# One decoder layer on one core: the third norm turned by DMA transposes instead of TensorE, with the router's product and the output sum reordered

## The chip, the cores and the metric

The kernel runs on one core of one Trainium2 chip. The metric is the device time of one execution in microseconds (us), the median of several runs. PE is TensorE, PEld its weight loads, DVE is VectorE, ACT is ScalarE, POOL is GpSimd and SP is SyncE, which issues the DMAs.

## What is computed

Eight sequences of 512 rows by 256 features go through one pre-norm decoder layer:

```
x = x + attn(layernorm(x))        # 16 heads; softmax over the sequence makes a Toeplitz matrix; W_V, W_O, bias
x = x + xattn(layernorm(x), ctx)  # causal cross attention, one head of width 256
x = x + ffn(layernorm(x))         # 2 shared experts and 16 routed ones (64 wide), top 2
# ffn: logits = flat @ router_w; the two largest of 16 are weighed (softmax) into comb
#      h = silu(flat @ wg) * (flat @ wu) * comb ; out = sum over experts of h @ wd
```

Products are computed in three fp16 passes on high and low halves (`three_passes`, L140), so each operand is kept as a high part (ACT copies to fp16) and a low part (the rest, a subtraction on DVE or POOL).

## The kernel before

**Staging.** One batch passes three stages in three consecutive iterations, so iteration `it` holds three batches at once: stage f of batch `it` (first norm, `z`, values), stage m of batch `it-1` (Toeplitz product, output projection, second norm, cross attention, third norm), stage d of batch `it-2` (router, gates, down products). `f, m, d, n` say which stages run; n is the first norm of the next batch. The iterations are 0 to 8, then `finish`. Iteration 0 has f alone and iteration 1 (`second_iteration`) has f and m together with much of the context work (`context(n, units)`: queries and values of the cross attention for batch n); 2 and 3 take the contexts 6 and 7; 4 to 6 are a hardware loop (`Fori`, L452 and PE's own at L2007); 7 has no n; 8 has no f and no n.

**Order.** Every engine has its own hand written program; all order between engines comes from semaphores. A wait holds up everything behind it on its engine. PSUM has three pairs of banks, `turned`, `score` and `rows`, each with a written order of its uses (L58 to L61); PE fills (`fill`) when the use two places before is taken, and DVE takes in that order (`take`, `reach`). Two more banks, `wide`, hold the Toeplitz sums, the contexts and, from `down(b, 0)` on, the output sums y.

**Gates.** For each of ten middle blocks j: PE makes g and u (`gate_up`, 12 matmuls of 512 columns, from h3T), ACT the tanh, DVE `open_gate` (and the product with `comb_rows`, L1252), DVE `pass_gate` (L1260), ACT the high part (L909), POOL the low part (L700), PE `down(j)` (12 matmuls of 256 columns). Block 9 is weighed after it is passed (`weigh_gate`, L1276).

**Third norm.** At j = 7 and j = 8 DVE normalises the halves of h3 (L1139). PE turns h3 in the middle of `gate_up(9)`, 8 transposes of 128x128 fp32 (L1638), between g9 and u9. ACT and DVE then part the turned banks into h3T (L813, L1149). The router's `logits` (L1691) and the next iteration's gates read h3T.

**End of an iteration on PE:** g9, turn h3, u9, `down(7)`, `z_product`, `down(8)`, `logits`, `down(9)`, then the next iteration's Toeplitz quarters. On DVE: pass and weigh block 9, part h3T, `z_max`, `route_top` (waits for the logits), `add_y` (waits for `down(9)`), then `route_rest` and the sums of the Toeplitz quarters. In iteration 8 `add_y` is left out and comes in `finish`, behind `route_top` and ahead of `route_rest`; PE's u0 there waits until DVE has counted two uses of `rows` past (L122), which DVE does behind `route_rest`.

**Second iteration, near its end.** PE: contexts 4, two halves of the turn of h3, `context(5, (0, 1))`, turn h1, `context(5, (2, 3))`. ACT and DVE part h3T, then the units of context 5, then h1T. ACT must wait for the store of context 2 before it writes unit 0 of context 5, which lies in the same buffer (`SAME_PAIR`, L66 and L881).

**Transfers.** SP already turns mix (two `DMA_TRANSPOSE` an iteration, L503) and h1 (one, L510). Its queue is in order.

## Time and profile before

| | us |
|---|---|
| median of 3 runs (lowest, highest) | 569.32 (568.86, 569.55) |
| the profiled execution's own time | 569.86 |
| its span, first to last instruction | 568.1 |
| PE busy | 542.3 (95%) |
| DVE busy | 424.9 (75%) |
| ACT busy | 257.4 (45%) |
| POOL busy | 201.2 (35%) |

A matmul's duration contains its way through the array, so consecutive matmuls overlap: the rate is read from start to start. In a timeline, a row is start, duration, engine, line, operation, output<-inputs, count, and in brackets the engine's idle time before it with what ended it. Iteration 1 begins at 33.84, 2 at 87.81, 3 at 155.67, 5 at 283.41, 6 at 343.90, 7 at 404.39, 8 at 464.46 (first Toeplitz matmul of each).

### The profile page before, as it was taken

The page shows a single profiled execution, that of the slowest core. Times are in us where ns is not written, and L with a number is a line of the kernel's source. Part 1 is how long each engine was busy: PE and PEld are TensorE (multiplying, and loading weights), DVE is VectorE, ACT ScalarE, POOL GpSimd, SP SyncE. Part 2 cuts the span into 40 slices and gives each one's busy share as a digit, 9 for nine tenths or more (in the row PEclk, how much of TensorE's full clock was granted, in tenths as well). Part 3 has the DMA queues.
Part 4 walks back from the last instruction along what each step waited for, and adds up shares of the span by engine and source line. Part 5 has one row for each costly group of instructions (what it writes and reads, how often), then busy time and mean ns, then how long its engine had stood idle before and what let it go on. Part 6 is the DMA issues. An engine that isn't in the chain of part 4 may idle for free. (4 is left out here: it accounts for less than half of the span.)

```text
span 568.1 us, 12928 instructions
## 1 busy us (share of the span) xinstructions
PE 542.3 (95%) x4716; PEld 369.6 (65%) x4716; DVE 424.9 (75%) x1101; ACT 257.4 (45%) x521; POOL 201.2 (35%) x246
## 2 busy tenths in 40 slices
PE   5799889999999999999999999999999998999997
PEld 4576557566776668666776668666866685666455
DVE  5867878778776697778886888678876876777654
ACT  4566657435354445435353545435543334332332
POOL 4225752214522154314512343334421343133123
PEclk9999989999999999999999999999999999999999
DMA  7988696793459823693459643994189216200341
GB/s 241 305 282 304 198 388 201 165 348 117 113 123 269 281 67 84 139 303 121 112 121 270 204 111 78 213 304 111 48 175 324 69 60 132 58 1 1 91 98 38
DMA packets 90734, 94.70 MB, mean 167 GB/s; under 512 B 28224, under 2 KB 76224, under 8 KB 90432
## 3 DMA queue, kind: packets, MB, share of 16 engines
q1 hardware_dynamic: 90688, 94.09, 58.7%
q8 instruction: 29, 0.48, 0.3%
q14 instruction: 17, 0.14, 0.1%
HBM read 75.66 MB, written 12.12 MB: 155 GB/s over the span
## 5 line engine op out<-in xcount | busy, mean ns | idle before, releaser
L700 POOL TENSOR_TENSOR mid<-gated,mid 128x512 f16<-128x512 f32 x72 | 86.4, 1200 | 214.2 <-ACT mid L909 214.1
L909 ACT ACTIVATE mid<-gated 128x512 f16<-128x512 f32 x72 | 45.0, 625 | 83.4 <-DVEq L1268 80.1
L142 PE MATMUL wide<-w_d,mid 128*128 128x256 f16 x288 | 78.5, 273 | 0.0
L144 PE MATMUL wide<-w_d,mid 128*128 128x256 f16 x288 | 78.5, 273 | 0.0
L143 PE MATMUL wide<-w_d,mid 128*128 128x256 f16 x288 | 78.5, 272 | 0.0
L1246 DVE SCALAR_TENSOR_TENSOR gated<-gated,score 128x512 f32<-128x512 f32 x72 | 49.2, 683 | 37.7 <-ACT gated L904 37.4
L142 PE MATMUL rows<-h3T,w_gu 128*128 128x512 f16 x160 | 60.7, 379 | 0.3 <-DVEq L122 0.3
L142 PE MATMUL score<-h3T,w_gu 128*128 128x512 f16 x160 | 60.7, 379 | 0.2
L143 PE MATMUL rows<-h3T,w_gu 128*128 128x512 f16 x160 | 60.6, 379 | 0.0
L144 PE MATMUL rows<-h3T,w_gu 128*128 128x512 f16 x160 | 60.6, 379 | 0.0
L144 PE MATMUL score<-h3T,w_gu 128*128 128x512 f16 x160 | 60.6, 379 | 0.0
L143 PE MATMUL score<-h3T,w_gu 128*128 128x512 f16 x160 | 60.6, 379 | 0.0
L904 ACT ACTIVATE gated<-score 128x512 f32<-128x512 f32 x72 | 42.3, 588 | 35.0 <-PE score L144 35.0
L1260 DVE SCALAR_TENSOR_TENSOR gated<-gated,rows 128x512 f32<-128x512 f32 x72 | 49.1, 682 | 7.5 <-PE rows L144 6.2
L890 ACT ACTIVATE prob<-score,s_bias 128x128 f32<-128x128 f32 (+3 forms) x32 | 16.9, 528 | 71.9 <-DVE s_bias L1213 71.9
L1252 DVE TENSOR_TENSOR gated<-gated,stage 128x512 f32<-128x512 f32 x49 | 33.9, 692 | 2.2 <-DMA stage<-comb_scratch 0.2
L142 PEld LDWEIGHTS wide<-w_d,mid 128*128 128x128 f16 x288 | 28.1, 98 | 10.1 <-issue 3.0
L143 PEld LDWEIGHTS wide<-w_d,mid 128*128 128x128 f16 x288 | 28.2, 98 | 5.8
L670 POOL TENSOR_SCALAR var_eps<-mean_var 128x2 f32<-128x2 f32 (+1 forms) x31 | 10.0, 323 | 61.0 <-DVE mean_var L1130 60.3
L144 PEld LDWEIGHTS wide<-w_d,mid 128*128 128x128 f16 x288 | 28.2, 98 | 3.3
L144 PEld LDWEIGHTS rows<-h3T,w_gu 128*128 128x128 f16 x160 | 15.7, 98 | 18.9
L144 PEld LDWEIGHTS score<-h3T,w_gu 128*128 128x128 f16 x160 | 15.7, 98 | 18.9
(251 smaller groups left out, 1423.5 us busy)
## 6 DMA issues: line engine op xcount, KB each, us to landing
toep<-z_scratch SPq DMA_DIRECT2D x14, 2048.0 KB, 18.0
stage<-comb_scratch SPq DMA_DIRECT2D x32, 512.0 KB, 8.4
toep<-z_scratch SPq DMA_DIRECT2D x4, 1024.0 KB, 10.3
x_bo<-in_x SPq DMA_DIRECT2D x8, 512.0 KB, 11.7
x_in<-in_xr SPq DMA_DIRECT2D x7, 512.0 KB, 11.1
qT<-q_scratch SPq DMA_DIRECT2D x7, 512.0 KB, 3.8
vx<-v_scratch SPq DMA_DIRECT2D x7, 512.0 KB, 5.1
out<-x_out SPq DMA_DIRECT2D x7, 512.0 KB, 3.3
```

Source lines behind the costliest of these rows:

```text
L142: pe.matmul(out, stationary[0], moving[0], start=start, stop=False, **kw)
L143: pe.matmul(out, stationary[0], moving[1], start=False, stop=False, **kw)
L144: return pe.matmul(out, stationary[1], moving[0], start=False, stop=stop, **kw)
L670: pool.tensor_scalar(var_eps[n][:, some], mean_var[n][:, some, 1], EPS, X_H ** -2, ALU.add, ALU.mult).then_inc(eps_added[n].sem, 1)
L700: pool.tensor_tensor(mid_slot(j, 1, late), gate_slot(j, late), mid_slot(j, 0, late), ALU.subtract).then_inc(mid_split.sem, 1)
L890: act.activation(prob[:, c % 2, 0:n], score.bank(score_use(it, c))[:, 0:n], ACT.Exp, bias=s_bias[:, c:c + 1], scale=1 / (X_Q * X_H), accum ...
L904: act.activation(gate_slot(j, late), score.bank(f"g{j}")[:], ACT.Tanh, scale=0.5 / (X_H * X_W)).then_inc(tanh_done.sem, 1)
L909: act.activation(mid_slot(j, 0, late), gate_slot(j, late), ACT.Copy).then_inc(mid_hi.sem, 1)
L1246: dve.scalar_tensor_tensor(to, to, 1.0, score.bank(f"g{j}")[:], ALU.add, ALU.mult).then_inc(score.taken.sem, 1)
L1252: dve.tensor_tensor(to, to, comb_rows[:, j - NSH], ALU.mult).then_inc(opened.sem, 1)
L1260: dve.scalar_tensor_tensor(to, to, X_MID / (2 * (X_H * X_W) ** 2), rows.bank(f"u{j}")[:], ALU.mult, ALU.mult).then_inc(rows.taken.sem, 1)
```

## The change

In iterations 2 to 7 h3 is no longer turned by PE. ACT copies the halves of h3 to fp16 in h2's buffer, DVE takes the low part of the first half and POOL that of the second, and SP turns high and low parts with one DMA transpose each, into h3T (odd iterations) or cT (even ones). Iterations 1 and 8 still turn on PE. On PE the logits go behind `down(9)`, on DVE `add_y` goes ahead of `route_top`. SP issues h1's transpose ahead of the fetch of the context. The iterations 4 to 6 are written out. In iteration 0 ACT and POOL part the columns of context 1 earlier; in iteration 1 ACT, DVE, POOL and PE are reordered.

```
+FIRST_MOVED = 2
...
-            with eng.Fori(2 + len(CONTEXT_IN), B - 1) as it:
+            for it in range(2 + len(CONTEXT_IN), B - 1):
                 iteration(it, True, True, True, True)
...
+            def move_h3(it, b):                                   # SP
+                if it == 2 or it == 4 and not h3_moved(2):
+                    sp.wait_ge(ctx_taken.sem, ctx_taken.at(6, UNITS))
+                sp.wait_ge(rows.ready.sem, rows.is_ready(it - 1, f"u{MID - 1}"))
+                parts_of = h2[:].rearrange("p c e -> p (c e)").bitcast(F16).rearrange("p (a n) -> p a n", a=2)
+                for a, made in enumerate((h3_hi, h3_split)):
+                    hold(sp, made, made.at(b, 2))
+                    sp.dma_start(h3T_of(it)[:, a].rearrange("p k (c s) -> p (k c) s", s=P), parts_of[:, a],
+                                 transpose=True).then_inc(h3T_moved.sem, 16)
...
+                if n and d:
+                    move_h1(it + 1)
                 if f and m:
                     fetch_context(it, it)
-                if n and d:
-                    move_h1(it + 1)
+                if h3_moved(it):
+                    move_h3(it, it - 1)
...
                 reciprocal_deviation(it - 1, 2)                   # POOL, second_iteration
+                part_context_columns(5)
                 reciprocal_deviation(it - 1, 2, 1)
-                part_context_columns(5)
...
                 for j in range(MID):                              # POOL
+                    if h3_moved(it) and j == MID - 2:
+                        part_h3(it - 1, 1)
                     if d and j:
                         part_mid(it - 2, j)
-                    if f and not m and j == 2:
+                    if f and not m and j == 0:
                         part_context_columns(1)
...
+                    if h3_moved(it - 1):                          # ACT, take_rest, q == 0
+                        act.wait_ge(h3T_moved.sem, h3T_moved.at(it - 2, 32))
...
-                exp_scores(it, it - 1, 2)                         # ACT, second_iteration
-                part_context_columns(4)
                 act.wait_ge(w_lo, GATES_2 + 1)
                 part_context(3, (2,))
                 part_prob(it, it - 1, 1)
+                exp_scores(it, it - 1, 2)
+                part_context_columns(4)
...
                 normalise_x(it + 1)
+                part_context(5, (0,))
                 part_turned(it, it - 1, h3T, h3T_hi, "h3")
-                part_context(5, (0, 1))
+                part_context(5, (1,))
...
                 if f and not m:                                   # ACT
-                    part_context(0, (0, 1))
                     part_context_columns(1)
-                    part_context(0, (2, 3))
+                    part_context(0, range(UNITS))
...
                 for j in range(AHEAD, MID):                       # ACT
+                    if h3_moved(it) and j == MID - 2:
+                        part_h3(it - 1, 0)
                     if d and j < MID - 1:
                         part_mid(it - 2, j - 1)
                     if d:
                         tanh(it, it - 2, j)
+                    if h3_moved(it) and j == MID - 2:
+                        part_h3(it - 1, 1)
...
-                if d and m:
-                    act.wait_ge(rows.ready.sem, rows.is_ready(it, f"u{MID - 1}"))
-                if m:
-                    part_turned(it, it - 1, h3T, h3T_hi, "h3")
+                if m and not h3_moved(it):
+                    part_turned(it, h3_turns(it), h3T_of(it), h3T_hi, "h3")
...
                     if m and at == C + 1:                         # DVE, j = 8
                         normalise(it - 1, it, 2, x_res, h3, 1)
+                        if h3_moved(it):
+                            part_h3(it - 1, 0)
                     if d:
                         open_gate(it, it - 2, j)
...
+                if d and it < B:                                  # DVE
+                    add_y(it - 2)
                 if d:
                     route_top(it + 1, it - 1)
-                if d and not (isinstance(it, int) and it == B):
-                    add_y(it - 2)
...
-                turn_halves(it, "h3", h3, h_ready[2], b)          # PE, second_iteration
-                context(5, (0, 1))
+                turn_halves(it, "h3", h3, h_ready[2], b, between=5)
+                context(5, (1,))
...
                         gate_up(it, j, some=slice(0, 1))          # PE
-                        turn_halves(it, "h3", h3, h_ready[2], it - 1)
+                        if not h3_moved(it):
+                            turn_halves(it, "h3", h3, h_ready[2], it - 1)
                         gate_up(it, j, some=slice(1, 2))
...
                 if d:
+                    down(it - 2, MID - 1)
                     turned.reach(pe, turned.ready, it)
                     rows.reach(pe, rows.ready, it)
                     logits(it + 1)
-                if d:
-                    down(it - 2, MID - 1)
```

`between=5` puts `context(5, (0,))` between the two halves of the turn. `part_h3` is one ACT copy of 128x512 fp32 to fp16, or one DVE or POOL `tensor_tensor` subtraction of two SBUF operands of that size. In the second iteration DVE also takes the statistics of x, the first two blocks, later, and unit 0 of context 5 ahead of h3T.

## Rows read from the trace of the kernel before

**Rows 1.** The page, busy time of each engine.
```profile
PE 542.3 (95%) x4716; PEld 369.6 (65%) x4716; DVE 424.9 (75%) x1101; ACT 257.4 (45%) x521; POOL 201.2 (35%) x246
```
**Rows 2.** Timeline of PE, end of iteration 5.
```profile
336.35 1.04 PE L1638 MATMUL turned<-ident,h 128*128 128x128 f32 x8
...
341.99 0.17 PE L142 MATMUL rows<-w_r,h3T 128*128 128x16 f16 x1
...
342.60 0.27 PE L142 MATMUL wide<-w_d,mid 128*128 128x256 f16 x1
...
343.90 0.22 PE L1752 MATMUL turned<-val,toep 128*128 128x128 f16 x1
```
**Rows 3.** Timelines of DVE, then ACT, then POOL, same place: block 9's way.
```profile
338.80 0.69 DVE L1260 SCALAR_TENSOR_TENSOR gated<-gated,rows 128x512 f32<-128x512 f32 x1 [0.93 <-PE rows L144]
339.59 0.69 DVE L1276 TENSOR_TENSOR gated<-gated,stage 128x512 f32<-128x512 f32 x1
...
340.31 0.63 ACT L909 ACTIVATE mid<-gated 128x512 f16<-128x512 f32 x1 [0.43 <-DVE gated L1276]
...
337.74 1.16 POOL L700 TENSOR_TENSOR mid<-gated,mid 128x512 f16<-128x512 f32 x1 [2.43 <-ACT mid L909]
341.02 1.16 POOL L700 TENSOR_TENSOR mid<-gated,mid 128x512 f16<-128x512 f32 x1 [2.12 <-ACT mid L909]
```
**Rows 4.** DMA view, the transposes: count, us from issue to landing.
```profile
mixT<-mix SPq DMA_TRANSPOSE x14, 3.2
...
h1T<-h1p SPq DMA_TRANSPOSE x5, 6.5
```
**Rows 5.** Timelines of DVE and POOL, iteration 5 at block 7, and in `finish`.
```profile
333.51 0.74 DVE L1139 TENSOR_SCALAR h<-x_res,mean_var,rstd 128x256 f32<-128x256 f32 x2 [0.16 <-DVE gated L1260]
...
334.16 1.16 POOL L700 TENSOR_TENSOR mid<-gated,mid 128x512 f16<-128x512 f32 x1 [0.84 <-ACT mid L909]
...
529.72 1.15 POOL L700 TENSOR_TENSOR mid<-gated,mid 128x512 f16<-128x512 f32 x1 [7.16 <-ACT mid L909]
...
529.81 1.15 DVE L1371 TENSOR_TENSOR comb<-comb 128x64 f32<-128x64 f32 x1
```
**Rows 6.** Timelines of DVE and PE, start of iteration 6: comb made and turned.
```profile
349.64 0.23 DVE L1371 TENSOR_TENSOR comb<-comb 128x64 f32<-128x64 f32 x1
...
350.64 0.60 PE L1799 MATMUL turned<-ident,comb 128*16 128x128 f32 x4
```
**Rows 7.** Timeline of POOL, end of iteration 7: block 9's low part.
```profile
461.93 1.16 POOL L700 TENSOR_TENSOR mid<-gated,mid 128x512 f16<-128x512 f32 x1 [2.06 <-ACT mid L909]
```
**Rows 8.** Timelines of DVE and PE, end of iteration 8 and `finish`.
```profile
525.55 0.16 DVE L1329 CAST top_f<-top_i 128x8 f32<-128x8 uint32 x1
...
525.67 0.39 PE L142 MATMUL rows<-h3T,w_gu 128*128 128x512 f16 x1 [0.27 <-DVEq L122]
```
**Rows 9.** Timelines of DVE, PE, SP and ACT, iterations 0 and 1.
```profile
23.03 3.05 DVE L1139 TENSOR_SCALAR x_in<-x_in,mean_var,rstd 128x256 f32<-128x256 f32 x4 [0.34 <-POOL rstd L673]
...
26.23 1.06 PE L1622 MATMUL turned<-ident,x_in 128*128 128x128 f32 x8 [1.29 <-PEq L122]
...
35.47 0.37 SPq L497 DMA_DIRECT2D x_bo<-in_x  x1
...
36.53 0.60 ACT L844 ACTIVATE h<-wide 128x512 f32<-128x512 f32 x1 [2.54 <-PE wide L144]
```
**Rows 10.** Timelines of DVE, PE and ACT, end of iteration 1.
```profile
75.51 2.40 DVE L1139 TENSOR_SCALAR h<-x_res,mean_var,rstd 128x256 f32<-128x256 f32 x2
...
77.96 0.66 PE L1638 MATMUL turned<-ident,h 128*128 128x128 f32 x4 [2.27 <-DVE h L1139]
...
81.28 0.60 ACT L885 ACTIVATE stage<-wide 128x512 f16<-128x512 f32 x1 [1.65 <-DMA v_scratch<-stage]
...
82.73 1.04 PE L1622 MATMUL turned<-ident,x_in 128*128 128x128 f32 x8
```
**Rows 11.** Windows: stretch, length, PE busy (x), PEld, DVE, ACT, POOL, PEclk, DMA share, GB/s.
```profile
79.00:80.00 1.00, 1.00 (x4) 0.38 (x3) 0.82 (x2) 0.63 (x2) 1.00 (x2) 0.50 0.99 406
```

More of the change, by code:

```diff
@@ L468, in mid_slot, with h3_moved, h3_turns, h3T_of @@
             return mid[:, half, j % SLOTS]
+        def h3_moved(it):
+            return FIRST_MOVED <= it < B
+        def h3_turns(it):
+            return sum(not h3_moved(i) for i in range(1, it))
+        def h3T_of(it):
+            return h3T if it % 2 else cT
+        def h3_rows(a):
+            return h2[:].rearrange("p c e -> p (c e)").bitcast(F16).rearrange("p (a k c e) -> p a c k e", a=2, k=K2, c=C)[
+                :, a]
         def context_unit(n, u, half):
@@ L830, in normalise_x, with part_h3 @@
                         last.then_inc(h_ready[0].sem, 1)
+            def part_h3(b, half):
+                act.wait_ge(h_ready[2].sem, h_ready[2].at(b, half + 1))
+                some = slice(2 * half, 2 * half + 2)
+                act.activation(h3_rows(0)[:, some], h3[:, some].rearrange("p c (k e) -> p c k e", k=K2),
+                               ACT.Copy).then_inc(h3_hi.sem, 1)
             def normalise_last(b, it):
@@ L1133, in normalise @@
             def normalise(b, it, n, src, dst, half=0):
-                if n and not half:
+                if n == 2 and not half and h3_moved(it - 1):
+                    dve.wait_ge(h3_split.sem, h3_split.at(b, 0))
+                elif n and not half:
                     dve.wait_ge(turned.ready.sem, turned.was_ready(it, f"h{n + 1}.1"))
@@ L1150, in part_turned, with part_h3 @@
                                       ALU.subtract).then_inc(turned.taken.sem, 1)
+            def part_h3(b, half):
+                dve.wait_ge(h3_hi.sem, h3_hi.at(b, half + 1))
+                some = slice(2 * half, 2 * half + 2)
+                dve.tensor_tensor(h3_rows(1)[:, some], h3[:, some].rearrange("p c (k e) -> p c k e", k=K2),
+                                  h3_rows(0)[:, some], ALU.subtract).then_inc(h3_split.sem, 1)
             def part_h1(b):
@@ L1567, in iteration @@
                     rows.reach(dve, rows.taken, it)
-                if m:
-                    part_turned(it, it - 1, h3T, h3T_hi, "h3")
+                if m and not h3_moved(it):
+                    part_turned(it, h3_turns(it), h3T_of(it), h3T_hi, "h3")
                 if n and d:
@@ L1624, in turn, with turn_halves @@
                     last.then_inc(turned.ready.sem, 1)
-            def turn_halves(it, use, src, made, b, second=None):
+            def turn_halves(it, use, src, made, b, second=None, between=None):
                 pe.wait_ge(turned.taken.sem, turned.is_free(it, f"{use}.1"))
@@ L1631, in turn_halves @@
                 for c in range(C):
+                    if c == 2 and between is not None:
+                        context(between, (0,))
                     if c % 2 == 0:
@@ L1692, in logits @@
                 rows.fill(pe, it, "logit")
-                pe.wait_ge(turned.taken.sem, turned.is_taken(it - 1, "h3.1"))
+                if h3_moved(it - 1):
+                    pe.wait_ge(h3T_moved.sem, h3T_moved.at(it - 2, 32))
+                else:
+                    pe.wait_ge(turned.taken.sem, turned.is_taken(it - 1, "h3.1"))
                 for q in range(C):
@@ L1696, in logits @@
                         last = three_passes(pe, rows.bank("logit")[:, NE * q:NE * q + NE],
[L1697 removed]
+                                            parts(h3T_of(it - 1), k, slice(P * q, P * q + P)), parts(w_r, k, slice(None)),
                                             start=(k == 0), stop=(k == K2 - 1))
@@ L1790, in gate_up @@
                                             parts(w_gu, k, slice(2 * P * j + at, 2 * P * j + at + P)),
-                                            parts(h3T, k, slice(None)), start=(k == 0), stop=(k == K2 - 1))
+                                            parts(h3T_of(it - 1), k, slice(None)), start=(k == 0), stop=(k == K2 - 1))
                     last.then_inc(banks.ready.sem, 1)
@@ L2006, in _ @@
                 iteration(it, True, True, True, True, c)
-            with pe.Fori(2 + len(CONTEXT_IN), B - 1) as it:
+            for it in range(2 + len(CONTEXT_IN), B - 1):
                 iteration(it, True, True, True, True)
```

22 lines of the change are left out of this document (15 added, 7 removed).

## The prediction

> **What bounds the kernel now.** I read the page first: PE is busy 95% of the span [rows 1], and the chain that ended last runs through PE nearly throughout. So anything taken off PE pays, until something else ends last at the same place. Next I read PE's timeline at the end of an iteration in the middle (5): every row starts where the one before lets it. I then followed block 9, the last that `down(9)` waits for, over DVE, ACT and POOL [rows 3]. It is ready at 341.02 + 1.16 = 342.18, and `down(9)` starts at 342.60 [rows 2]: a margin of 0.42 us, which is what decides here. Last I read the three places where PE does stand still: the start of iteration 1, the end of iteration 1 and the hand-over to `finish` [rows 8 to 10].
>
> **The turn of h3, iterations 2 to 6.** PE loses 8 transposes, from 336.35 to the next matmul, 8 x 0.109 = 0.87 us [rows 2]. Block 9's u comes that much earlier, and its way to POOL takes as long as before, so it is ready at 342.18 - 0.87 = 341.31. PE would want it, with the logits (341.99 to 342.60, 0.61 us) no longer in front of `down(9)`, at 341.99 - 0.87 = 341.12. That is a stall of about 0.2 us, with 0.05 for the semaphore. So the logits behind `down(9)` cost part of what the turn gives. A second loss: DVE's weighing of block 9 moves from 339.59 to 338.72, while POOL's low part of block 8 runs from 337.74 to 338.90 and isn't moved [rows 3]. Both read two SBUF operands. In `finish` such a pair took 1.15 us on DVE (a 128x64 product that takes 0.23 alone, by the same timeline) while POOL ran from 529.72 to 530.87 [rows 5]: DVE waited for POOL. So 0.2 us more. What remains is 0.87 - 0.25 - 0.2 = 0.4 us per iteration.
>
> **The added work.** ACT: two copies of about 0.6 us, as large as L909 [rows 3], for two that go; at block 8 ACT is free, nothing. POOL: one more L700-sized subtraction, 1.16 us, between blocks 7 and 8, where it idles 2.43 us before 337.74 [rows 3]; nothing. DVE: one subtraction of 0.7 us between the second normalising (333.51) and `open_gate(8)`, for two that go at the end. Here is the open price. The new subtraction would start at about 334.17, when the two normalisings let it, and POOL starts block 7 at 334.16 [rows 5]. If DVE gets in first, POOL and then DVE's own L1252 move by some 0.6 us and I put 0.2 us more on block 9; the gain is then 0.2 to 0.25 us an iteration. The other case is the first rival. Five iterations: **-1.2 us**; bounds +1.9 (rival) and 5 x -0.87 = -4.4.
>
> **Transfers.** A transpose of 256 KB lands 3.2 us after its issue, h1's of twice the size 6.5 [rows 4]. High parts can go at 335.2 and low parts at 336.6, so both are there by 339.9, or by 343.1 at the larger price; the logits now come at about 342.7. On SP, h1's transpose goes first and the context's fetch behind it, which nobody needs before the next iteration's scores, 20 us on. Taken at nothing; at the larger price the logits wait 0.4 us in an iteration. If this cover went, the logits and `route_top` would be late next.
>
> **The order behind it.** `add_y` waits for `down(9)`, now ahead of the logits, and `route_top` waits for the logits; DVE ends about 0.2 us later relative to the Toeplitz quarters. Who waits for it is the turn of comb, which has 0.8 us to spare (comb is made at 349.87, turned at 350.64 [rows 6]). Nothing. Unrolling: iterations 2, 3 and 7 are already written out and show no stall of PE of their own; nothing, and at most 0.2 us either way.
>
> **Iteration 7** has no `z_product` to cover the wait. Block 9 is ready at 461.93 + 1.16 = 463.09 [rows 7], 0.87 earlier 462.22; PE would be there at 461.2. So the stall of 1.1 us eats the turn and the 0.48 us that the logits waited for h3T before. `down(9)` at 462.27, 1.31 us, logits 0.61: Toeplitz at 464.2 against 464.46, less the port: **-0.15 us** (bounds +0.35, -0.87).
>
> **Iteration 8 and `finish`** still turn on PE, but the logits move behind `down(9)` too. Block 9 is ready just when `down(9)` starts today, so the logits start not at 522.01 but 1.92 later (1.31 + 0.61). DVE's `route_top`, `add_y` and `route_rest` (to 525.7) follow them in that order, and PE's u0 waits for DVE to count past behind `route_rest`: it starts at 525.67 [rows 8] and will start at 527.6. PE cannot pass it, and what follows is chained: **+1.9 us** (bounds +1.3, if half a microsecond is taken up later, and +2.2).
>
> **Iteration 0.** PE waits 1.29 us before h1's turn at 26.23, for four normalisings that take 3.05 us beside POOL's low parts of context 1 [rows 9]; a pair of the same instruction takes 0.74 elsewhere [rows 5]. The change moves POOL's work to before them, so 1.4 us go. But the second half of the Toeplitz product needs a transfer that SP sees landed at 35.47, and it starts at about 36.45 today (ACT takes the first half at 36.53) [rows 9]. So 0.95 at most: **-0.9 us** (bounds 0, -1.4).
>
> **Iteration 1.** PE waits 2.27 us for the second half of h3 (two normalisings in 2.40 us beside POOL), and behind it the clock granted drops to half, 1.2 instead of 2.4 GHz, from 78.8 to 82.3 [rows 10, 11]; 8 matmuls of 512 columns cost 0.21 more each, 1.7 us. The change fills the gap with `context(5, (0,))`, 1.3 us, and moves POOL's work; h3 is turned at about 77.8 instead of 78.5. But ACT now has unit 0 of context 5 in front of h3T, and it must wait for a store that landed at 81.28 [rows 10]. Today h3T is parted right behind the turn, ahead of that wait. After: unit 0 81.9, the two halves of h3 by 82.9 on ACT and 83.9 on DVE, which has unit 0 first; PE's turn of h1 needs those banks, so it ends at 84.3, not at 83.6, and PE idles from 79.2 to 83.15. That is +0.7, and a wait longer than today's should bring the half clock again: +1.2 on top of today's, since its cost now lies behind the wait. **+1.9 us** (bounds +2.4, and -1.7 if the clock stays and the store is early).
>
> **The sum:** -0.9 + 1.9 - 1.2 - 0.15 + 1.9 = +1.55 us, on a profiled execution of 569.86 (span 568.1). The median of the runs shown is 569.32, half a microsecond less; I add the sum to it: 570.9.
>
> **Rivals.** *POOL gets the port at block 7.* Then DVE's new subtraction waits for 335.3, `open_gate(8)` starts at 335.8 instead of 334.60, pass 8 and with it block 8's low part slip by 1.2 us, weighing 9 waits for that (339.8), and block 9 is ready at 342.3: the Toeplitz quarters start 0.4 us later than today, five times, and 0.35 in iteration 7. That is 3.6 us more than the sum: 574.5. For it: the starts are 334.16 against 334.17, and where POOL started 0.09 us ahead it won [rows 5]. Against: the normalisings on DVE hold on just before. The Trainium skill (SBUF — State Buffer, the terms and "SBUF: two separate sides") says that DVE and GpSimd share a port pair as an exclusive lock, taken by whichever starts first for the whole instruction, also by a DVE operation with two SBUF inputs; by that rule, the trace agrees in the pair of 1.15 us, and this rival's time would be the answer.
>
> *The end of iteration 1 isn't held.* If the store lands before ACT comes to it, or ACT's wait is short, h3T and h1T follow the turn at once, PE has no gap, and the clock stays up: from there on the place gives 1.7 us instead of costing 1.9, and the total is 570.9 - 3.6 = 567.3, faster. It decides if the store lands before about 79.5. For it: iteration 0's gain moves it to 80.4. Against: everything in front of it moves too, and the transfers ahead of it are one long queue.
>
> *The turn's 0.87 us isn't replaced by a stall* (block 9 comes earlier than I chain it): 5 x 0.6 more, about 568, within 0.2% to faster.
>
> **Chances.** Forecast (570.4 to 573) 0.40, first rival (573 to 576) 0.22, second 0.20, third 0.18. About 0.2%, 1.1 us, is what a measurement can tell from no change. Of the forecast 0.10 lies within it, of the third 0.08: faster 0.28, same 0.18, slower 0.54. The range takes in both rivals' times: 566.8 to 575.2.
>
> **What would show it.** Turns of h3 on PE: 16, not 64 matmuls. Right: a stall of PE before `down(9)` in iterations 2 to 6 of 0.2 to 0.6 us, and of 1 us in iteration 7; u0 in `finish` 1.7 us after g0's end; ACT idle on the store ahead of unit 0 of context 5; the half clock again near 85. Wrong: Toeplitz starts of iterations 4 to 6 under 60.0 or over 60.7 us apart, L700 or DVE's new subtraction at its plain length where I see a clash, or no half clock.

## The result and the profile after

The changed kernel takes 571.81 us (median of 12 runs, 570.23 to 573.17), the kernel before 569.70 us on the same chip (12 runs, 568.86 to 570.56): ratio 1.0035, 95% interval 1.0025 to 1.0045. It is slower by 0.35%, within the range and 0.9 us above the time predicted. Between the two profiled spans lie 1.5 us (569.6 against 568.1), where the sum had 1.55; that is closer than its terms are, and luck (below). One run of experiment 11 took 787.41 us at a mean granted clock of 0.657, while all others here lie between 562 and 579 us; its ratio leaves that run out.

First the busy times from the page, then PE, DVE, POOL and ACT at the end of iteration 5, from their timelines (start, duration; lines have moved: L144 to L146 are the three passes, L1705 turns h3, L1211 and L735 are the new subtractions, L1314 weighs block 8, L1338 block 9):

```profile
PE 539.9 (95%) x4668; PEld 365.2 (64%) x4668; DVE 418.8 (74%) x1095; ACT 258.0 (45%) x521; POOL 213.5 (37%) x252
```
```profile
341.28 0.27 PE L146 MATMUL wide<-w_d,mid 128*128 128x256 f16 x1
341.77 0.28 PE L144 MATMUL wide<-w_d,mid 128*128 128x256 f16 x1 [0.21 <-POOL mid L741]
...
334.34 0.69 DVE L1211 TENSOR_TENSOR h<-h 128x512 f16<-128x512 f32 x1
...
335.66 0.93 DVE L1314 TENSOR_TENSOR gated<-gated,stage 128x512 f32<-128x512 f32 x1
...
339.02 0.79 DVE L1338 TENSOR_TENSOR gated<-gated,stage 128x512 f32<-128x512 f32 x1
...
334.34 1.71 POOL L741 TENSOR_TENSOR mid<-gated,mid 128x512 f16<-128x512 f32 x1 [0.84 <-ACT mid L961]
336.00 1.60 POOL L735 TENSOR_TENSOR h<-h 128x512 f16<-128x512 f32 x1
...
340.56 1.15 POOL L741 TENSOR_TENSOR mid<-gated,mid 128x512 f16<-128x512 f32 x1 [1.29 <-ACT mid L961]
```

Against [rows 1] PE has 48 matmuls less: 8 transposes in each of six iterations. Against [rows 2] the turn is gone, and between the matmuls at 341.28 and 341.77 stands a wait: a start-to-start of 0.49 where 0.11 is the rate, so 0.38 us. It ends when POOL has block 9's low part. Against [rows 3], block 9's way itself (weigh, ACT, POOL) is as long as before but for 0.10 us in L1338. At block 7 [rows 5] POOL and DVE now start in the same hundredth, 334.34; DVE's subtraction takes its plain 0.69 us and POOL's 1.16 becomes 1.71. Behind it DVE's L1314 takes 0.93 for 0.69 and POOL's L735, as large as L741, takes 1.60.

The place that costs is the end of iteration 1, against [rows 10, 11]: the timelines of ACT, DVE and PE, and three one-microsecond windows (busy times, then PE's granted clock as a share, DMA share, GB/s).

```profile
80.33 0.60 ACT L937 ACTIVATE stage<-wide 128x512 f16<-128x512 f32 x1 [3.16 <-DMA v_scratch<-stage]
80.83 1.08 ACT L856 ACTIVATE h3T<-turned 128x512 f16<-128x512 f32 x2
...
80.96 0.69 DVE L1266 SCALAR_TENSOR_TENSOR stage<-wide,stage 128x512 f16<-128x512 f32 x1 [4.46 <-ACT stage L937]
...
82.40 0.63 PE L1687 MATMUL turned<-ident,x_in 128*128 128x128 f32 x4 [3.93 <-DVE h3T L1204]
```
```profile
84.00:85.00 1.00, 1.00 (x7) 0.69 (x6) 1.00 (x2) 0.29 (x1) 0.00 (x0) 0.50 0.48 193
85.00:86.00 1.00, 1.00 (x6) 0.70 (x5) 0.01 (x1) 0.00 (x0) 0.00 (x0) 0.50 0.07 29
86.00:87.00 1.00, 1.00 (x7) 0.79 (x6) 0.12 (x1) 0.60 (x1) 0.00 (x0) 0.63 0.00 0
```

ACT stands 3.16 us on a store, h3T waits behind it, PE waits for h3T, and then PE runs at half the clock (1.2 instead of 2.4 GHz). At the other end, in `finish`, against [rows 8]:

```profile
525.26 0.38 PE L146 MATMUL score<-cT,w_gu 128*128 128x512 f16 x1
527.16 0.39 PE L144 MATMUL rows<-cT,w_gu 128*128 128x512 f16 x1 [1.51 <-DVEq L124]
```

u0 starts at 527.16, 1.68 us after it could (start to start 1.90, rate 0.22). Cut at the first Toeplitz matmul of each iteration, as before (us; iteration 4 left out; the last three columns are experiments 2, 3 and 10):

| stretch | before | after | logits first | both edits | best |
|---|---|---|---|---|---|
| start of iteration 1 | 33.84 | 32.72 | 32.15 | 32.74 | 32.06 |
| iteration 1 | 53.97 | 56.54 | 55.70 | 52.99 | 51.94 |
| iteration 2 | 67.87 | 67.77 | 68.05 | 68.83 | 67.84 |
| iteration 3 | 67.14 | 66.59 | 66.23 | 66.21 | 66.22 |
| iteration 5 | 60.49 | 59.98 | 59.58 | 59.57 | 59.59 |
| iteration 6 | 60.49 | 59.97 | 60.66 | 60.52 | 59.99 |
| iteration 7 | 60.07 | 59.88 | 59.29 | 59.62 | 59.29 |
| 8 and `finish`, to PE's last | 99.84 | 102.25 | 100.25 | 100.46 | 100.36 |

### The profile page after: what moved, and what is told of

It is laid out like the page before. It is cut to its first block and busy times, and to the rows that moved or that the text cites. A ratio compares the mean times of both kernels' runs of the same rounds, so it can differ in the third digit from the quotient of the medians.

```text
span 569.6 us, 12271 instructions
## 1 busy us (share of the span) xinstructions
PE 539.9 (95%) x4668; PEld 365.2 (64%) x4668; DVE 418.8 (74%) x1095; ACT 258.0 (45%) x521; POOL 213.5 (37%) x252
## 5 line engine op out<-in xcount | busy, mean ns | idle before, releaser
L741 POOL TENSOR_TENSOR mid<-gated,mid 128x512 f16<-128x512 f32 x72 | 89.9, 1248 | 199.0 <-ACT mid L961 199.0
L144 PE MATMUL wide<-w_d,mid 128*128 128x256 f16 x288 | 78.6, 273 | 2.9 <-POOL mid L741 2.9
L146 PE MATMUL wide<-w_d,mid 128*128 128x256 f16 x288 | 78.5, 273 | 0.0
L144 PEld LDWEIGHTS wide<-w_d,mid 128*128 128x128 f16 x288 | 28.1, 98 | 15.1 <-POOL mid L741 5.1
L1314 DVE TENSOR_TENSOR gated<-gated,stage 128x512 f32<-128x512 f32 x49 | 35.3, 721 | 1.8
L145 PEld LDWEIGHTS wide<-w_d,mid 128*128 128x128 f16 x288 | 28.2, 98 | 5.8
L144 PE MATMUL rows<-cT,w_gu 128*128 128x512 f16 x80 | 30.3, 379 | 1.5 <-DVEq L124 1.5
L144 PE MATMUL score<-cT,w_gu 128*128 128x512 f16 x80 | 30.3, 379 | 0.2
L144 PE MATMUL rows<-h3T,w_gu 128*128 128x512 f16 x80 | 30.3, 379 | 0.0
L145 PE MATMUL rows<-h3T,w_gu 128*128 128x512 f16 x80 | 30.3, 379 | 0.0
L146 PE MATMUL rows<-h3T,w_gu 128*128 128x512 f16 x80 | 30.3, 379 | 0.0
L145 PE MATMUL rows<-cT,w_gu 128*128 128x512 f16 x80 | 30.3, 379 | 0.0
L146 PE MATMUL rows<-cT,w_gu 128*128 128x512 f16 x80 | 30.3, 379 | 0.0
L146 PE MATMUL score<-cT,w_gu 128*128 128x512 f16 x80 | 30.3, 379 | 0.0
L145 PE MATMUL score<-h3T,w_gu 128*128 128x512 f16 x80 | 30.3, 379 | 0.0
L146 PE MATMUL score<-h3T,w_gu 128*128 128x512 f16 x80 | 30.3, 379 | 0.0
```

Of the source, the lines that this page charges most:

```text
L144: pe.matmul(out, stationary[0], moving[0], start=start, stop=False, **kw)
L145: pe.matmul(out, stationary[0], moving[1], start=False, stop=False, **kw)
L146: return pe.matmul(out, stationary[1], moving[0], start=False, stop=stop, **kw)
L741: pool.tensor_tensor(mid_slot(j, 1, late), gate_slot(j, late), mid_slot(j, 0, late), ALU.subtract).then_inc(mid_split.sem, 1)
L1314: dve.tensor_tensor(to, to, comb_rows[:, j - NSH], ALU.mult).then_inc(opened.sem, 1)
```

## The experiments

Each edit is made in the changed kernel unless another is named. The kernel before ran beside every group: 569.62 us (experiments 1 to 4), 569.48 (5, 6, 8, 9), 569.81 (7, 10, 11) and 569.79 (12), each on another chip. The changed kernel's 571.81 comes from the first comparison, beside 569.70, so a difference to it holds within some 0.3 us. The profile of each kernel is of one execution.

**1. h3T parted ahead of context 5, on ACT and DVE.**

```diff
-                part_context(5, (0,))
                 part_turned(it, it - 1, h3T, h3T_hi, "h3")
-                part_context(5, (1,))
+                part_context(5, (0, 1))
```

> The end of iteration 1 alone: ACT and DVE part h3T ahead of unit 0 of context 5, so nothing that PE's turn of h1 needs stands behind the store that ACT waits for until 80.31. Theory (that wait cost the 4.09 us of PE idle, and the idle brought the granted clock of 0.50 behind it): PE idles under 1 us there, no slice at 0.50 between 83 and 87, iteration 1 goes from 56.54 to 52 to 53.5 us, the median falls by 3 to 4.5 us, to about 568, below the kernel before. Rival (PE then has nothing to do but wait for the loads and for context 5 anyway, so the gap only moves behind h1's turn): iteration 1 stays above 55 us and the median within 1 us of 571.8. All later iterations as in the changed kernel, 59.98 us for iterations 4 to 6.

569.48 us (567.81 to 570.82, 12 runs), ratio to before 0.9991 (0.9979 to 1.0003): 2.3 us won, less than the 3 to 4.5 expected. Iteration 1 takes 54.92. The gap went behind h1's turn, as the rival has it, but shorter:

```profile
78.72 1.16 PE L1685 MATMUL turned<-ident,x_in 128*128 128x128 f32 x8
81.90 0.28 PE L144 MATMUL wide<-w_vx,w_q_k 128*128 128x256 f16 x1 [2.02 <-DVE stage L1265]
```

Both theories hold in part. The order cost PE time; and behind it stands the same store, since unit 2 of context 5 needs the bank that unit 0 leaves only when the store (landed at 80.50 here) lets ACT write `stage`. The clock still fell, from 83.0 to 86.4.

**2. The logits ahead of the last down product, route_top ahead of add_y.**

```diff
                 if d:
-                    down(it - 2, MID - 1)
                     turned.reach(pe, turned.ready, it)
                     rows.reach(pe, rows.ready, it)
                     logits(it + 1)
+                    down(it - 2, MID - 1)
```

> The logits back ahead of the last down product, and route_top ahead of add_y on DVE; h3 stays turned by transfers. Theory (the move behind the last down product costs 1.9 us in iteration 8 and finish, and in iterations 2 to 6 it only leaves PE a wait of 0.38 us): iteration 8 and finish fall from 102.25 to about 100.3 us, iterations 4 to 6 from 59.98 to between 59.6 and 59.9, iteration 7 from 59.88 to about 59.3, in all 2.5 to 4.5 us less, about 568.5. Rival (the logits, moved forward, wait for the transfers of h3, which land at 340.75 at the latest, with the casts of ACT and DVE behind them, up to 343): a wait of 0.5 to 1.5 us ahead of the logits in iterations 2 to 7, iterations 4 to 6 at 60.4 to 61, so that the 1.9 us of the finish are given back and the median is 571 to 574.

569.07 us (567.26 to 570.92, 12 runs), ratio 0.9992 (0.9980 to 1.0004), 2.7 us under the changed kernel. Iteration 8 and `finish` fall by 2.00 us, to within 0.4 of before, as this experiment's theory had it. Iteration 5 takes 59.58, against 60.49 before: all of the turn's 0.87 us, and no wait. But in iterations 2 and 6 the logits wait, 1.09 and 1.05 us, and there the rival is right:

```profile
398.88 0.27 PE L146 MATMUL wide<-w_d,mid 128*128 128x256 f16 x1
400.05 0.17 PE L144 MATMUL rows<-w_r,cT 128*128 128x16 f16 x1 [0.89 <-DMA cT<-h]
```

The second transpose of h3 lands 3.0 to 3.1 us after its issue in iterations 3, 4, 5 and 7, and 4.6 us in 2 and 6. The changed kernel has the same two late ones (4.37 and 4.46 us); its logits come late enough not to notice. The DMA view of the changed kernel, from 337 to 342 and from 397 to 402 (queue: packets, MB, share of 16 engines):

```profile
q1 hardware_dynamic: 1792, 0.44, 47.9%
```
```profile
q1 hardware_dynamic: 1751, 0.43, 84.4%
q8 instruction: 1, 0.02, 1.2%
q14 instruction: 1, 0.01, 0.4%
```

The same bytes take 1.8 times the engine time, in stretches in which packets of the instruction queues are seen. No experiment was made on this, but all traces agree. The 12 profiles with such transposes hold 144 of them. In the time of 25 a packet of queue 8 starts: 22 of these took 4.37 to 4.87 us, one 4.20 and two 3.1. Of the other 119 one took 4.21 and the rest 3.0 to 3.8. The lateness isn't tied to the iteration either. Experiments 6 and 11 add matmuls to PE's program; in both, the second transposes of iterations 2 and 6 take 3.1 us and have no such packet, and in experiment 11 the late ones with a packet are the second of iteration 4 (4.46) and the first of iteration 5 (4.43). So the time goes with that packet, and its place with the program. That the packet itself is what delays the transpose isn't shown.

**3. Both edits.**

> Both edits together. If the two places are independent, the gains add: the median falls by 5.5 to 8.5 us from 571.8, to about 565, 0.6 to 1 per cent below the kernel before. If the logits wait for the transfers, only the gain at the end of iteration 1 is left, about 568. If neither theory holds, within 1 us of 571.8.

566.11 us (565.29 to 566.85, 5 runs), ratio 0.9933 (0.9919 to 0.9946). The gains add: 2.3 and 2.7 make 5.0, 5.7 measured. PE's waits at the end of iteration 1 are 0.50 and 0.58 us, and the clock stayed up there. But it had been at half from 66.4 to 69.8, where PE had idled 2.2 us, and so PE came later to the end of the iteration. In experiments 1 and 9, whose iteration 1 is written the same, the clock was up at 67 and fell at the end instead, and the iteration took 54.92 and 54.68 us against 52.99 here. So with one order the stretch differs by 1.9 us between executions, by where the clock falls.

**4. Without the transfers.**

```diff
-FIRST_MOVED = 2
+FIRST_MOVED = 8
```

> Everything of the change but the transfers: h3 is turned by PE in all iterations, the logits still behind the last down product. Theory (the transfers give what iterations 4 to 6 gained, 0.5 us each in iterations 2 to 6 and little in 7; the turn of 0.87 us is in part replaced by a wait of 0.38): iterations 4 to 6 back at 60.5 us, the stall ahead of the last down product gone, the median 2 to 3.2 us above the changed kernel, about 574.4. Rival (the gain comes from the order, the logits behind the last down product, and not from the transfers): iterations 4 to 6 within 0.15 us of 59.98 and the median within 0.8 us of 571.8.

576.89 us (576.65 to 578.69, 4 runs), ratio 1.0133 (1.0114 to 1.0151), 5.1 us above the changed kernel. Iterations 4 to 6 take 60.71 each, and the wait ahead of the last down product is not gone, as I had expected it to be, but 0.23 us (iteration 5, from start to start 0.34 where 0.11 is the rate):

```profile
344.05 0.27 PE L146 MATMUL wide<-w_d,mid 128*128 128x256 f16 x1
344.39 0.28 PE L144 MATMUL wide<-w_d,mid 128*128 128x256 f16 x1
```

This closes the account of an iteration. The logits' move alone makes a wait of 0.23 us, which is what the order costs against before (60.71, 60.49). The transfers take 0.87 us of turning off PE and lengthen the wait by 0.15, so they are worth 0.72; read from the stretches, 0.73 (60.71, 59.98). Iterations 2 to 6 together differ by 3.2 us, the upper end of what was expected. Most of the rest is one wait in iteration 7, where DVE stood 1.12 us for a transfer of comb and PE 1.16 us behind it; that stretch is 1.67 us longer, and I had not sized it.

**5. Iteration 0 as before.** The edit is on POOL and ACT (the expectation names the engines wrongly):

```diff
-                    if f and not m and j == 0:
+                    if f and not m and j == 2:
                         part_context_columns(1)
...
+                    part_context(0, (0, 1))
                     part_context_columns(1)
-                    part_context(0, range(UNITS))
+                    part_context(0, (2, 3))
```

> The changed kernel with iteration 0's order of POOL and DVE as it was before, and nothing else. Theory (the new order lets PE turn h1 earlier, and half of that is handed back at the wait for the second half of the Toeplitz transfer): PE starts iteration 1 at 33.8 instead of 32.7, and the Toeplitz wait of 0.44 us is gone. What of these 0.7 us reaches the end depends on the store that ACT waits for at the end of iteration 1: if that store's transfer is queued behind transfers that don't move with PE, nothing reaches the end and the median stays within 0.4 us of 571.8; if it moves, the median rises by 0.7. I lean to the first, since the queue is busy without a gap there (share over 1.0 from 64 to 84).

570.69 us (569.32 to 575.30, 12 runs), ratio to before 1.0032 (1.0011 to 1.0052). The interval holds that of the changed kernel, so the medians leave it open whether this edit is worth anything. The profile tells more. DVE and PE, then DVE of the changed kernel:

```profile
22.18 3.05 DVE L1195 TENSOR_SCALAR x_in<-x_in,mean_var,rstd 128x256 f32<-128x256 f32 x4 [0.34 <-POOL rstd L707]
...
25.38 0.84 PE L1688 MATMUL turned<-ident,x_in 128*128 128x128 f32 x6 [1.28 <-PEq L124]
```
```profile
23.39 1.38 DVE L1194 TENSOR_SCALAR x_in<-x_in,mean_var,rstd 128x256 f32<-128x256 f32 x4 [0.35 <-POOL rstd L707]
```

PE's wait of 1.28 us [rows 9] is back, and iteration 1 starts at 32.99, against 31.88 to 32.15 in the six profiles (experiments 2 and 6 to 10) with the new order and full clock in iteration 0. So 0.8 to 1.1 us are won there by this reading. It rests on one profile of the old order: that of the kernel before, with the same order and the clock also up, starts iteration 1 at 33.84, 0.85 us later still. What the runs show for sure is the wait that comes and goes with the order. What becomes of the time won hangs on the second half of the Toeplitz transfer. Where PE found it landed (experiments 6 and 9) the store at the end of iteration 1 lands at 79.4; where PE waited for it (1.13 us in experiment 2) the store lands at 80.57, and here, with the old order, at 80.47. My leaning was wrong in its reason: the queue in front of the store begins with the Toeplitz transfers of iteration 1, which wait for PE's product, and the store lands 19.4 to 19.5 us after their issue in the changed kernel and in experiments 1, 2, 3, 5, 6 and 9 alike. It moves with PE.

**6. Matmuls that nobody reads, in the gap of iteration 1.**

```diff
                 context(5, (1,))
+                pe.wait_ge(rows.taken.sem, rows.is_taken(it, "o2"))
+                for n in range(60):
+                    pe.matmul(rows.bank("o2")[:, 0:P], ident16[:], future[:], start=True, stop=True,
+                              skip_group_check=True)
                 pe.wait_ge(h_ready[0].sem, h_ready[0].at(it + 1, 2))
```

> The changed kernel with 60 matmuls of 128x128 added, whose output nobody reads, between unit 1 of context 5 and PE's turn of h1, that is in the 4 us in which PE had nothing to do. They take 3.3 us at 0.055 us each, so they end before the turn can start. Theory (the granted clock falls to 0.50 after PE's idle, and the matmuls behind it pay for it): no slice at 0.50 between 83 and 87, 1.5 to 1.8 us less from the turn of h1 to iteration 2, and the median down by 1.2 to 1.8 us, to about 570.2. Rival (the half clock there doesn't depend on what PE did in the gap): it stays at 0.50 for 3.3 us and the median is within 0.4 us of 571.8.

570.41 us (569.24 to 571.84, 12 runs), ratio 1.0015 (1.0004 to 1.0026): 1.4 us under the changed kernel by the medians and 1.1 by the ratios to the kernel before, about what the theory has. Timeline of PE, then a window, at the place:

```profile
77.29 3.51 PE L1945 MATMUL rows<-future,ident 128*128 128x128 bf16 x60
81.45 0.41 PE L1687 MATMUL turned<-ident,x_in 128*128 128x128 f32 x2 [0.65 <-DVE h3T L1204]
```
```profile
84.00:85.00 1.00, 1.00 (x12) 0.90 (x10) 0.44 (x2) 0.56 (x1) 0.00 (x0) 1.00 0.07 29
```

From the turn of h1 to iteration 2 it is 5.19 us (81.45 to 86.64) instead of 6.86 (82.40 to 89.26): 1.67 us, with the same work in between and the clock up. The mean granted clock of each run says that this is no single lucky execution. Of the changed kernel's 12 runs none is above 0.997; the 8 at 0.994 have a median of 572.21 us and the 4 at 0.997 one of 570.38. With the gap filled, 4 of 12 runs are at 0.999 or 1.0 and 3 at 0.993.

**7. Both low parts of h3 on POOL.**

```diff
@@ POOL
                     if h3_moved(it) and j == MID - 2:
+                        part_h3(it - 1, 0)
                         part_h3(it - 1, 1)
@@ DVE
                         normalise(it - 1, it, 2, x_res, h3, 1)
-                        if h3_moved(it):
-                            part_h3(it - 1, 0)
```

> The changed kernel with both low parts of h3 made on POOL, so that DVE's new subtraction is gone from the spot where it and POOL's low part of block 7 started together at 334.34. Theory (the meeting of the two engines there costs 0.55 us of POOL and 0.24 us of DVE, but block 9's way to the last down product starts with PE's own matmuls, which end at 338.1, so none of it is on the path): POOL's low part of block 7 goes from 1.71 back to 1.16 us, DVE's weighing of block 8 from 0.93 to 0.69 us, and iterations 4 to 6 stay at 59.98 within 0.1 us; the median is within 0.5 us of 571.8. Rival (the meeting is what makes the wait of 0.38 us ahead of the last down product): iterations 4 to 6 at 59.6 to 59.8, six iterations together 1.5 to 2 us. A second rival: POOL's two subtractions of 1.16 us push its low part of block 8 (338.11 now) later by up to 0.8 us, weighing of block 9 meets it on DVE, and the iterations take 60.1 to 60.6 us.

573.98 us (572.12 to 576.28, 6 runs), ratio 1.0067 (1.0046 to 1.0089), 2.2 us above the changed kernel. Iteration 5 takes 60.54, inside the second rival's range, with 0.94 us of wait ahead of the last down product. But the meeting that costs most is another than that rival's: it is at the weighing of block 8 (L1315), not of block 9. Timelines of DVE and POOL, iteration 5:

```profile
336.65 1.66 DVE L1315 TENSOR_TENSOR gated<-gated,stage 128x512 f32<-128x512 f32 x1
338.34 0.69 DVE L1323 SCALAR_TENSOR_TENSOR gated<-gated,rows 128x512 f32<-128x512 f32 x1
...
336.60 2.72 POOL L735 TENSOR_TENSOR h<-h 128x512 f16<-128x512 f32 x2
339.83 1.16 POOL L741 TENSOR_TENSOR mid<-gated,mid 128x512 f16<-128x512 f32 x1 [0.51 <-ACT mid L962]
```

POOL starts its subtraction at 336.60, DVE its weighing (two SBUF operands) at 336.65, and DVE takes 1.66 us for what takes 0.69. That is the mechanism of the prediction's first rival: the engines start 0.05 us apart here, 0.00 in the changed kernel. The Trainium skill (SBUF — State Buffer, "SBUF: two separate sides") gives the port pair to whichever engine starts first for a whole instruction; here POOL led by 0.05 us and won, and DVE took 0.97 us longer where POOL's plain 1.16 less the lead would be 1.11, so the trace agrees but for 0.14 us. In the changed kernel, at equal starts, DVE won. DVE's L1323 reads PSUM too and ran its plain 0.69 us beside POOL.

**8. The stores of contexts 2 and 3 ahead of x_bo's transfer**, in the kernel of experiment 3.

```diff
                 if f and m and not d:
-                    load_residual(it)
...
                     store_context(2)
                     store_context(3)
+                    load_residual(it)
                     load_context(6)
```

> The kernel with both edits, and one more: in iteration 1 the transfer of x_bo (1.46 us of the queue, landing at 77.81) is issued behind the stores of contexts 2 and 3 instead of ahead of them. Theory (the end of iteration 1 is set by the landing of context 2's store at 80.3, which waits its turn in one full queue): that store lands 1.4 us earlier, unit 0 of context 5 starts at about 78.8 instead of 80.15, and iteration 2 starts at about 84.5 instead of 85.73, so the median is 1.0 to 1.5 us under the 566.1 of the kernel with both edits. Rival (something else is right behind it, POOL's bias on x_bo, 2.9 us, or ACT's own work to 79.6): 0 to 0.4 us.

565.93 us (563.94 to 567.74, 6 runs), ratio 0.9931 (0.9908 to 0.9954). In the profile the theory holds: the store lands 18.0 us after the issue of the Toeplitz transfers instead of 19.4, ACT starts unit 0 of context 5 at 78.51, iteration 1 takes 52.16 instead of 52.99 (this profile has the clock up all through, that of experiment 3 not, so the 0.83 isn't the edit's alone).

```profile
78.51 1.08 ACT L936 ACTIVATE stage<-wide 128x512 f16<-128x512 f32 x2 [0.75 <-DMA v_scratch<-stage]
```

The medians (565.93 against 566.11) can't show it; the runs lie 4 us apart.

**9. The logits behind only in iterations 2 and 6**, in the kernel of experiment 3.

```diff
+LOGITS_BEHIND = (2, 6)
...
+                    if it in LOGITS_BEHIND:
+                        down(it - 2, MID - 1)
...
                     logits(it + 1)
-                    down(it - 2, MID - 1)
+                    if it not in LOGITS_BEHIND:
+                        down(it - 2, MID - 1)
```

> The kernel with both edits, but the logits stay behind the last down product in iterations 2 and 6, the two in which h3's second transpose took 4.4 to 4.6 us to landing instead of 3.1 and the logits waited 1.16 and 0.94 us for it. Theory: the wait there becomes the one of 0.38 us ahead of the last down product, iteration 2 loses 0.8 us less and iteration 6 0.6 us less, and the median is 1.2 to 1.5 us under 566.1. Rival (the slow transposes aren't tied to these iterations, or the wait moves to the next one): within 0.4 us of 566.1.

565.86 us (563.87 to 570.02, 10 runs), ratio 0.9935 (0.9913 to 0.9957). Iteration 6 goes from 60.52 to 59.96 and iteration 2 from 68.83 to 67.62 (0.4 of it from a shorter wait in project_mix, the output projection), so the theory holds where it is read; the median is inconclusive, for the same reason. The choice of iterations 2 and 6 is tied to this program: in experiment 11 the late transpose is in iteration 4, and the logits wait there (0.74 us of idle, iteration 4 at 60.50 instead of 60.21 in experiment 10).

**10. Experiments 3, 8 and 9 together.**

> All the edits that gained: h3 parted ahead of context 5, the logits ahead of the last down product except in iterations 2 and 6, and the stores of contexts 2 and 3 ahead of x_bo's transfer. If the gains seen in the profiles add (0.8 us for the store, 1.4 us for the order in iterations 2 and 6), 564.5 us, 0.9 per cent under the kernel before. If the medians of the two kernels with one of these edits each are the truth (0.2 us each), 565.8.

563.80 us (563.22 to 564.78, 4 runs), ratio 0.9897 (0.9881 to 0.9912). This beats both kernels, by 6.0 us and 8.0 us, and lies nearer the sum of the gains (564.5) than that of the medians (565.8). Its stretches are the last column above.

**11 and 12. Matmuls nobody reads in iteration 0 too, then at the end of iteration 1 only.** To experiment 10 the first adds 30 behind the first turn of h1 and 12 behind the turn of h1 in iteration 1; the second has the 12 alone.

```diff
             turned.reach(pe, turned.ready, -1)
+            for n in range(30):
+                pe.matmul(wide[:, 0, 0:P], ident16[:], future[:], start=True, stop=True, skip_group_check=True)
```

> The same, with matmuls of 128x128 whose output nobody reads in two places where PE idles: 30 behind the first turn of h1, where PE otherwise waits 2.2 us and the granted clock was at 0.50 from 11 to 15 in four of ten profiles so far, and 12 behind the turn of h1 at the end of iteration 1. Theory (the granted clock falls only after such an idle, in some executions and not in others, and this is a good part of the spread of 3 us and more between executions of one kernel): no slice at 0.50 in iteration 0, iteration 1 starts at 31.9 to 32.2 us, the median falls by 0.5 to 1 us against the same kernel without them, and the highest run comes down. Rival (what the clock costs in iteration 0 is taken up by the store that iteration 1's end waits for, or the spread comes from elsewhere): the median within 0.3 us and the spread as wide.

> The kernel of all the gains with only the 12 matmuls at the end of iteration 1, not the 30 in iteration 0. With both it took 567.9 us against 563.8 without either, though no slice of its profile was at half the clock; transfers landed late there: the second half of the Toeplitz matrices at 35.83 instead of 34.79, x_bo at 42.26 instead of 39.16, and PE waited 2.06 us at 47.46. Theory (the 30 matmuls in iteration 0 are what costs: their place shifts the code and transfers of the start): this kernel is at 563 to 564.5 us, x_bo lands near 39.2. Rival (the 12 at the end of iteration 1 cost it, by pushing context 5 behind them): about 567 us, with x_bo at 39.2. Third: it is also at 566 to 568 with x_bo landing late, so that the start differs from kernel to kernel or run to run for a reason that neither edit holds.

With both: 567.88 us (10 runs, 564.67 to 569.24 but for the one of 787.41), ratio 0.9951 (0.9927 to 0.9975), 4 us worse than without. With the 12 alone: 564.35 us (562.85 to 566.84, 4 runs), ratio 0.9896 (0.9880 to 0.9913), the same as without. So the 30 cost. The clock theory is not borne out: the profile has no slice at half clock, but 8 of the 13 profiles with PE idle there have none in iteration 0 either, and of the nine runs 6 have a mean granted clock of 0.994 or 0.997, 3 one of 1.0. Nor was time won: iteration 1 still starts at 32.08, the second half of the Toeplitz matrices lands at 35.83 instead of 34.79 and x_bo at 42.26 instead of 39.16, and PE waits 1.28 and 2.06 us for them. Why the transfers were later isn't settled. In the profile of the second x_bo lands at 40.22 and the Toeplitz half at 36.19, with half clock from 11 to 14 (it is of the slowest of the four runs, 566.84 us), so landing times at the start differ for more than one reason.

## Why the prediction was right, point by point

The terms were off by -0.2 us (iteration 0), +0.7 (iteration 1), -1.0 (iterations 2 to 6), 0.0 (iteration 7) and +0.5 (the end). They cancel to -0.1: that the sum is so near the measured 1.5 is luck, while the signs of all five are borne out, and but for the port the mechanisms. Of the 0.9 us between 570.9 and 571.81, 0.4 is the kernel before, at 569.70 in these runs and 569.32 in those that I added the sum to. (The chances don't add up as stated: by their own parts they are 0.30 for faster and 0.52 for slower, not 0.28 and 0.54.)

**End of iteration 1 (+1.9).** Right in mechanism, too small: iteration 1 is 2.57 us longer. ACT's wait for the store ahead of h3T, PE idle behind it (4.09 us) and the half clock behind that are all there. PE's wait is 0.1 us from the forecast (79.2 to 83.15). Experiment 6 puts the clock at 1.67 us where I had counted 1.2 as new; the 0.47 between them is about what iteration 2's start is off (below). Experiment 1 gives 2.3 us for the order. The other rival, "the end isn't held", fell: the store landed at 80.31, against a forecast of 80.4 and the 79.5 it needed. What I did not see is that the store holds the end of the iteration by itself, through `stage` and the banks; experiments 1 and 8 show it. In the kernel before it doesn't reach PE: ACT waits for the store [rows 10], but PE starts unit 2 at 83.61 without a wait, 1.0 us after DVE is done with unit 0. By my estimate PE would have come 1.7 us earlier and waited, had the clock not been at half, so part of that half clock was hidden. Timelines of DVE and PE there, in the kernel before:

```profile
81.91 0.69 DVE L1204 SCALAR_TENSOR_TENSOR stage<-wide,stage 128x512 f16<-128x512 f32 x1 [1.45 <-ACT stage L885]
...
83.61 0.27 PE L142 MATMUL wide<-w_vx,w_q_k 128*128 128x256 f16 x1
```

**Iteration 0 (-0.9).** Right in mechanism: DVE's four normalisings take 1.38 us instead of 3.05 and PE's wait before h1's turn is gone, and it is back in experiment 5. Iteration 1 starts 1.12 us earlier, the wait for the second half of the Toeplitz transfer takes 0.44 back, and the store lands 0.95 earlier than before (80.31, 81.26). The size depends on the execution and rests on single profiles: this one had the granted clock at half from 11 to 15, and others had a Toeplitz wait of 0 to 1.1 us (experiment 5). The two terms together were to be +1.0; iteration 2 starts 1.45 us later (89.26, 87.81), 0.45 more, which the dearer clock accounts for.

**Turn of h3, iterations 2 to 6 (-1.2).** Right sign, mis-sized: 0.52 us an iteration in 4 to 6 where I had 0.25, in all 2.2 us. Two of the three stretches (59.98, 59.97) lie just under the 60.0 that I had named as a sign of being wrong. The stall came as forecast (0.38 for "0.2, with 0.05", and up to 0.6 was allowed; 0.23 of it without the transfers, experiment 4). The step that failed is the port, charged twice at 0.2 us. At block 7 DVE won, POOL lost 0.55 us and DVE's L1314 0.24 behind it, but block 9's way starts with PE's matmuls that end near 338.1, so nothing of that is on it; at block 8 it cost 0.10. The rows of `finish` show what a meeting costs the engine that waits; they can't show how much of it reaches PE. The transfers cost nothing in this order, as I had taken: the later one of iteration 5 is issued at 337.69 and lands at 340.74, and the logits start at 343.09. In iteration 2 only 0.10 us came: PE's wait in project_mix went from 0.41 to 0.92 us.

**Iteration 7 (-0.15).** -0.19, with the stall of 1.12 us ahead of the last down product that was put at 1.1.

**Iteration 8 and `finish` (+1.9).** +2.41. The move alone is 2.0 (experiment 2). The rest is PE's waits in project_mix, 0.91 and 0.59 against 0.47 and 0.45, which no step of mine contained; their cause is open (SP issues the first transpose of mix there 0.45 us after POOL's part ended, in the kernel before 0.10 us after it).

**The rivals.** POOL with the port at block 7 did not come, at a tie of 0.00 us; its price is real (experiment 7). "The turn's 0.87 isn't replaced by a stall" is false for this order and true for the other (experiment 2, iteration 5): the stall is made by the logits' move (0.23 us with the turn still on PE, experiment 4) and not by the turn. That is the plain answer to where the gain went. The transfers bring 0.7 to 0.9 us an iteration; the logits behind the last down product hand back 0.4 in each and 2.0 at the end, and the reordering of iteration 1 hands back 2.3.

## What to carry to other kernels

When work is taken off the engine that bounds, look which of its own pieces stood ahead of the next late operand: the logits were the cover for block 9's way, and moving them uncovered it. Before moving a piece behind a wait on a store, follow that store's transfer through its queue to what opens the queue, and let the work that needs its landing stand behind all that doesn't. Judge such edits by the stretch that they touch in a profile, and only their union by the median: two edits of 0.8 and 1.4 us were not visible alone at 4 to 6 us of spread. And look at the granted clock of each profile before comparing a stretch of two: the same iteration 1 took 52.99, 54.68 and 54.92 us.

## What the runs showed that was not expected

The granted clock falls in some executions and not in others after the same idle. PE idles 2.2 us in iteration 0 in every profile but that of experiment 11; the clock was then at half from 11 to 15 in 5 of these 13. It fell behind the idle of 2.2 us between 64 and 69 in 6 of the 13 profiles of changed kernels (in the kernel before PE idles 1.6 us there, and it stayed up). At the end of iteration 1 it stayed up behind 2.8 us (experiments 2, 5 and 7, in which it had fallen near 68), fell behind 2.2 us (experiments 1 and 9, in which it had not), and fell behind 2.7 us in experiment 4, in which it had. With the idle filled it stayed up in the profiles of experiments 6 and 11; the clocks of all runs bear this out for experiment 6 and not for 11.

h1's transpose, 6.5 us to landing before [rows 4], takes 4.3 us now that the context's fetch is issued behind it, while those of h3, half its size, take 3.1 to 3.5:

```profile
cT<-h SPq DMA_TRANSPOSE x6, 3.5
h3T<-h SPq DMA_TRANSPOSE x6, 3.1
h1T<-h1p SPq DMA_TRANSPOSE x5, 4.3
```

So the 6.5 us that I took as the price of size were in part the place in the queue, and the dearer bound for the transfers (343.1) was too dear.
